# Decoder of two layers: the last joint attention's products in high and low parts, its inputs in a ring by key head

## The chip, the core and the metric

The kernel runs on one core of a Trainium2 chip. TensorE (PE) multiplies, VectorE (DVE), ScalarE (ACT) and GpSimd (POOL) work element by element, SyncE (SP) issues most of the DMAs. The metric is the device time of the whole program in microseconds, as the median of repeated runs.

## What is computed

A decoder of two layers on x of shape (8, 112, 512), each with a self-attention, an attention to a context of 375 rows per batch, and a mixture of experts. The change concerns the second layer's attention to context and own tokens together (joint attention): 16 query heads and 4 key heads of width 128, so that four query heads share a key head. Cut to what matters:

```python
kv_in = jnp.concatenate([context_hidden, draft_hidden], axis=1)      # 375 + 112 = 487 rows
q = _rope(_rms_norm(q, q_norm_w), draft_position_ids)                # (8, 16, 112, 128)
k = _rope(_rms_norm(k, k_norm_w), full_position_ids)                 # (8, 4, 487, 128)
scores = jnp.einsum('bhqd,bhkd->bhqk', q, jnp.repeat(k, 4, axis=1)) * SCALE
probs = jax.nn.softmax(scores, axis=-1)
attn = jnp.einsum('bhqk,bhkd->bhqd', probs, jnp.repeat(v, 4, axis=1))
return attn.transpose(0, 2, 1, 3).reshape(bsz, draft_len, H * HD) @ Wo.T
```

## The kernel before

The program is a row of segments. In one segment several parts run interleaved: each part is a generator per engine, and an order, written out as a list of names ("a" the attention, "o" its output product and norm, "w" the splitting of Wo), says whose next piece is issued. Every engine gets its instructions in that order and executes them in that order.

The segment "joint4" has JointAttentionPart as "a". One item is a query head (128 in all), a step takes two (W), a group is the four heads of a key head (32 in all). Each step has two half-steps. In step s, the first half-step has on TensorE the transposes (L1920) of the two heads of step s - 2 and the scores (L1928) of the two heads of step s; the second has, in odd steps, the value product of a closed group (L1940). VectorE takes in the first half-step the reciprocal of the sums (L1953), and per head the maximum (L1958) and its negative (L1960). ScalarE copies the transposed heads from PSUM (L1974, L1975) in the first and takes the exponentials (L1981) in the second half-step. GpSimd multiplies the exponentials of the step before with the reciprocals (L1907) in the first half-step. Scores and value product are plain float32, which shows in the trace as two passes for each instruction. The transposed heads alternate between two banks (N_T), so a transpose waits until the head two before it has been taken out (pt_ready). SP loads q, k and v of a whole batch ahead, into two slots each.

The output part OutNormPart ("o") takes 46 pieces, five for each batch. Four of the five hold the product of one group with Wo in high and low parts: twelve products of 512 columns (L2238, L2240, L2242). Its input is split by ScalarE (oT_hi, L2121) and VectorE (oT_lo, L2171). One piece of the five has no product but the addition to x and the statistics of the batch (L2182, L2139, L2140, L2191), another ends with the transposes of the normed rows (L2252) and their split (hT_hi, hT_lo L2159). In the order, an "o" follows the first half-step of each even step, and one more follows the second half-step of every eighth step, so TensorE has, for one group: transposes, scores, output product, transposes, scores, value product. The segment before, "p4", makes q, k and v, and loads those of the first batch at its end (FirstBatchPart).

Of the kernel before, what the change touches and what calls it, by code (L numbers as in the profile page):

```python
# [20 lines left out]
F32 = mybir.dt.float32  # L21
# [8 lines left out]
B = 8  # L30
# [1803 lines left out]
class JointAttentionPart:  # L1834


    def __init__(self, g, name, q_at, k_at, v_at, key_chunks, scale, s_banks, t_banks, o_bank, tiles):
        core, ps = g.core, g.ps
        dh, n_items, W, group = 128, 16, 2, 4
        S, nch = sum(key_chunks), len(key_chunks)  # L1840
        offs = [sum(key_chunks[:c]) for c in range(nch)]
        n_steps, n_groups = n_items // W, n_items // group
        RING, LT, LP = 3 * W, 2, 2
        LE = LP
        N_S, N_T = len(s_banks), len(t_banks)
        n_all = B * n_steps
        self.steps, self.lead, self.turned = 2 + 2 * (n_all + LE), 2 * LE, True
        q, k, v = tiles
        p = g.sb(f"{name}_p", [T, RING, S])
        pt = g.sb(f"{name}_pt", [128, 2, nch, group, T])  # L1850
# [4 lines left out]
        qk_in, v_in = g.sems(f"{name}_qk_in", 2), g.sems(f"{name}_v_in", 2)  # L1855
        s_done, mx_ready, neg_ready, exp_done, rinv_ready, p_ready, t_done, pt_ready, pv_done = (
            g.sem(f"{name}_{n}") for n in ("s_done", "mx_ready", "neg_ready", "exp_done", "rinv_ready", "p_ready", "t_done",
                                           "pt_ready", "pv_done"))
        self.ot_done, self.o_used = pv_done, None
        n_k = len(k_at(0))  # L1860
# [10 lines left out]

        def ot_view(i):
            return ps[:, o_bank, 0:group * T].rearrange("p (c t) -> p c t", c=group)
        self.ot_view = ot_view

        def sync(sp):
            yield

            def load_qk(b):
                u = b % 2  # L1880
                reuse(sp, s_done, (b - 1) * n_items)
                sp.dma_start(q[:, u, :, :], q_at(b).rearrange("(c p) t -> p c t", p=128)).then_inc(qk_in[u], 16)
# [3 lines left out]
            def load_v(b):  # L1886
                reuse(sp, pv_done, (b - 1) * n_groups)
                for c, (n, src) in enumerate(zip(key_chunks, v_at(b))):
                    sp.dma_start(v[0:n, b % 2, c, :], src).then_inc(v_in[b % 2], 16)
            yield  # L1890
            for step in range(n_all + LE):
                b, n = step // n_steps + 1, step % n_steps
                if b < B and n == (1 if b == 1 else 0):
                    load_qk(b)
                if b < B and n == LP:
                    load_v(b)
                yield
                yield

        def gpsimd(pool):  # L1900
            yield
            yield
            for step in range(n_all + LE):
                for i in items(step, 1):
                    r = i % RING
                    pool.wait_ge(rinv_ready, i // W + 1)
                    pool.tensor_tensor(p[:, r, :], p[:, r, :], rinv[:, r:r + 1].to_broadcast([T, S]), ALU.mult).then_inc(p_ready, 1)  # L1907
                yield
                yield

        def tensor(pe):
            yield
            yield
            for step in range(n_all + LE):
                for t in items(step, LT):
                    pe.wait_ge(p_ready, t + 1)
                    reuse(pe, pt_ready, t - N_T + 1)
                    for c in range(nch):
                        n = key_chunks[c]
                        last = pe.transpose(ps[0:n, t_banks[t % N_T], c * T:(c + 1) * T], p[:, t % RING, offs[c]:offs[c] + n],  # L1920
                                            core.ident[0:T, 0:T])
                    last.then_inc(t_done, 1)
                for i in items(step):
                    b, h = i // n_items, i % n_items
# [6 lines left out]
                gr = closed(step, LP, group // W)  # L1931
                if gr is not None:
                    b, j = gr // n_groups, gr % n_groups
                    if j == 0:
                        reuse(pe, v_in[b % 2], (b + 1) // 2 * 16 * nch)
                    pe.wait_ge(pt_ready, (gr + 1) * group)
                    reuse(pe, self.o_used, gr)
                    for c in range(nch):
                        n = key_chunks[c]
                        last = pe.matmul(ps[:, o_bank, 0:group * T], v[0:n, b % 2, c, j * dh:(j + 1) * dh],  # L1940
# [1695 lines left out]
```

## Time and profile before

| | |
|---|---|
| median of 3 runs | 2760.98 us (2760.76 to 2762.0) |
| profiled execution | 2759.17 us, span 2757.5 us |
| PE busy | 2506.5 us (91%) |
| DVE / ACT / POOL busy | 1666.1 (60%) / 1132.2 (41%) / 935.4 us (34%) |
| joint scores L1928, PE | 256 passes, 118.6 us, 586 ns each |
| joint value products L1940, PE | 256 passes, 102.5 us, 543 ns each |
| joint transposes L1920, PE | 512 passes, 66.0 us, 271 ns each |
| joint exponentials L1981, ACT | 128, 85.5 us, 668 ns each |

Busy time of PE overlaps: matmuls are pipelined and their ends are modelled, so starts tell more than lengths. Rows of the timeline give the start and the length in us, then engine and line, output<-inputs and the number of merged instructions, and in brackets the idle time before them and what released it.

### The profile page before, as it was taken

How to read it: one execution, taken by the hardware profiler on the slowest of the kernel's cores; microseconds unless marked ns; L12 is line 12 of the kernel's file. 1: busy time of each engine (PE TensorE's matmuls, PEld its weight loads, DVE VectorE, ACT ScalarE, POOL GpSimd, SP SyncE). 2: the span in 40 equal slices, each digit the busy share in tenths (PEclk: the TensorE clock that was granted, in tenths of full speed). 3: DMA queues.
4: the chain of work that ended last, by engine and by line, in shares of the span. 5: the costliest groups of instructions: out<-in, count | busy, mean ns of one | idle time of the engine just before them, and what ended most of it. 6: DMA issues, size and time to landing. Idle time of an engine off the chain costs nothing. (4 is left out here: it accounts for less than half of the span.)

```text
span 2757.5 us, 48350 instructions
## 1 busy us (share of the span) xinstructions
PE 2506.5 (91%) x14891; PEld 2011.7 (73%) x14892; DVE 1666.1 (60%) x3141; ACT 1132.2 (41%) x2442; POOL 935.4 (34%) x942
## 2 busy tenths in 40 slices
PE   7999788779899999799997998988999999899998
PEld 7888666558688777588875886765666577788887
DVE  4536747669677566576665566864444435666564
ACT  2113266623333234455453233755555522444343
POOL 4213101134233235323333213743333412355554
PEclk9999989989899989899998999999999989999999
DMA  5454132136521046477774432353212031666664
GB/s 190 156 143 104 27 101 71 42 98 182 170 66 55 26 136 194 150 213 217 195 220 104 127 72 84 114 172 95 86 53 92 6 129 60 171 159 157 157 161 74
DMA packets 289278, 332.88 MB, mean 121 GB/s; under 512 B 147446, under 2 KB 202694, under 8 KB 287313
## 3 DMA queue, kind: packets, MB, share of 16 engines
q1 hardware_dynamic: 217904, 252.57, 29.2%
q0 software_dynamic: 20640, 51.74, 9.6%
q10 hardware_dynamic: 50560, 26.34, 3.3%
q8 instruction: 100, 1.64, 0.2%
q14 instruction: 74, 0.60, 0.1%
HBM read 233.86 MB, written 96.72 MB: 120 GB/s over the span
## 5 line engine op out<-in xcount | busy, mean ns | idle before, releaser
L898 PE MATMUL e_psum<-e_up_hi,hT_hi 128*128 x672 | 245.9, 366 | 21.5 <-DVE hT_lo L867 16.3
L900 PE MATMUL e_psum<-e_up_hi,hT_lo 128*128 x672 | 237.2, 353 | 0.0
L899 PE MATMUL e_psum<-e_up_lo,hT_hi 128*128 x672 | 237.0, 353 | 0.0
L1907 POOL TENSOR_TENSOR joint_a_p<-joint_a_p,joint_a_rinv 112x487 f32<-112x487 f32 x128 | 125.4, 1001 | 197.8 <-DVE joint_a_rinv L1953 197.5
L1567 POOL TENSOR_TENSOR self_a_p<-self_a_p,self_a_mx 112x448 f32<-112x448 f32 x96 | 96.1, 1001 | 207.8 <-DVE self_a_mx L1624 207.8
L898 PEld LDWEIGHTS e_psum<-e_up_hi,hT_hi 128*128 128x128 f32 x672 | 127.9, 190 | 44.3 <-issue 32.7
L1958 DVE TENSOR_REDUCE joint_a_mx<-joint_psum 112x1 f32<-112x487 f32 x128 | 84.9, 664 | 122.3 <-PE joint_psum L1928 121.9
L794 ACT ACTIVATE e_gate<-e_psum 128x352 f32<-128x352 f32 (+1 forms) x86 | 44.5, 517 | 258.9 <-PE e_psum L900 258.4
L873 DVE TENSOR_TENSOR hT_lo<-e_psum,hT_hi 128x256 fp32r<-128x256 f32 (+2 forms) x138 | 55.6, 435 | 143.2 <-ACT hT_hi L812 143.2
L1658 ACT ACTIVATE self_a_p<-self_a_p 112x448 f32<-112x448 f32 x128 | 71.6, 575 | 167.7 <-POOL self_a_p L1567 114.7
L1209 POOL TENSOR_TENSOR p_p_z<-p_p_straight,p_p_crossed 128x512 f32<-128x512 f32 x70 | 98.5, 1408 | 112.3 <-DVE p_p_crossed L1191 110.4
L900 PEld LDWEIGHTS e_psum<-e_up_hi,hT_lo 128*128 128x128 f32 x672 | 127.8, 190 | 11.8
L899 PEld LDWEIGHTS e_psum<-e_up_lo,hT_hi 128*128 128x128 f32 x672 | 128.2, 191 | 9.8
L828 DVE TENSOR_TENSOR e_up_lo<-e_up_raw,e_up_hi 128x1024 f32 (+3 forms) x128 | 127.8, 1050 | 3.7 <-issue 3.4
L847 DVE SCALAR_TENSOR_TENSOR e_act_raw<-e_gate,e_rows,e_psum 128x352 f32<-128x352 f32 (+1 forms) x86 | 55.3, 644 | 121.2 <-ACT e_gate L794 119.8
L766 POOL DMA_INDIRECT out<-e_y,e_back x51 | 120.2, 2357 | 17.3 <-issue 17.3
L752 POOL TENSOR_TENSOR e_held<-e_zeros 1x1 f32<-1x1 f32 x90 | 20.8, 231 | 302.3 <-DVE e_idx L862 302.3
L898 PE MATMUL e_psum<-e_dn_hi,hT_hi 128*128 (+1 forms) x285 | 120.3, 422 | 1.3 <-issue 0.7
L1928 PE MATMUL joint_psum<-x_first,x_q 128*112 128x487 f32 x256 | 118.6, 586 | 1.8 <-PEq L89 1.7
L142 PE MATMUL p_psum<-p_p_w_hi,hT_hi 128*128 128x512 f32 x280 | 115.5, 412 | 1.9 <-DVE p_p_w_lo L1175 1.9
L1981 ACT ACTIVATE joint_a_p<-joint_psum,joint_a_neg 112x487 f32<-112x487 f32 x128 | 85.5, 668 | 76.5 <-DVE joint_a_neg L1960 73.4
L781 ACT ACTIVATE e_up_hi<-e_up_raw 128x1024 f32 (+3 forms) x128 | 107.7, 923 | 15.1 <-PEq L89 15.1
(565 smaller groups left out, 7397.1 us busy)
## 6 DMA issues: line engine op xcount, KB each, us to landing
e_up_raw<-in_L_ffn_w SPq DMA_DIRECT2D x64, 512.0 KB, 5.1
e_up_raw<-in_L_ffn_w SPq DMA_DIRECT2D x64, 352.0 KB, 3.5
e_dn_raw<-in_L_ffn_w SPq DMA_DIRECT2D x16, 1024.0 KB, 5.5
q_all<-p_p_t_stage ACTq DMA_DIRECT2D x56, 256.0 KB, 2.3
e_dn_raw<-in_L_ffn_w SPq DMA_DIRECT2D x16, 512.0 KB, 4.1
x_q<-q_all SPq DMA_DIRECT2D x8, 896.0 KB, 5.4
v_ctx<-front_c_v_stage SPq DMA_DIRECT2D x24, 250.0 KB
x_others<-k_ctx SPq DMA_DIRECT2D x8, 750.0 KB, 5.1
```

The costliest lines, as they stand in the source:

```text
L142: last = pe.matmul(out, a, b, start=(k == 0 and i == 0), stop=(k == n_k - 1 and i == len(pairs) - 1))
L766: pool.indirect_dma_start(out=acc, out_offset=bass.IndirectOffsetOnAxis(ap=back[:, v, :], axis=0), in_=y[:, v, :], in_offset=None, compute ...
L781: act.activation(up_hi[:, bass.ds(slot * KC + k, 1), :], up_raw[:, k:k + 1, :], ACT.Copy).then_inc(up_hi_ready, 1)
L828: dve.tensor_tensor(up_lo[:, bass.ds(slot * KC + k, 1), :], up_raw[:, k:k + 1, :], up_hi[:, bass.ds(slot * KC + k, 1), :].bitcast(F32), AL ...
L898: pe.matmul(out, lhs[0], rhs[0], start=k == 0, stop=False)
L899: pe.matmul(out, lhs[0], rhs[1], start=False, stop=False)
L900: return pe.matmul(out, lhs[1], rhs[0], start=False, stop=k == n_k - 1)
L1209: both = pool.tensor_tensor(z[:, r, :], straight[:, r, :], crossed[:, r, :], ALU.add)
L1567: pool.tensor_tensor(p[:, i % RING, :, :], p[:, i % RING, :, :], mx[:, i % RING, :].unsqueeze(2).to_broadcast([T, group, T]), ALU.subtract ...
L1907: pool.tensor_tensor(p[:, r, :], p[:, r, :], rinv[:, r:r + 1].to_broadcast([T, S]), ALU.mult).then_inc(p_ready, 1)
L1928: pe.matmul(ps[0:T, s_banks[i % N_S], 0:S], q[:, b % 2, h, :], k[:, b % 2, h // group, :], start=True, stop=True).then_inc(s_done, 1)
L1981: act.activation(p[:, r, :], ps[0:T, s_banks[i % N_S], 0:S], ACT.Exp, bias=neg[:, r, :], scale=scale, accum_out=rsum[:, r:r + 1]).then_inc ...
```

## The change

Scores and value products are each made of three float32r products: high x high, high x low, low x high. The high parts of q, k and v are made by ScalarE, the low parts by GpSimd (group 0's q and k by VectorE). The transposed heads get their high part from ScalarE and their low part from VectorE, in the second half-step. q, k and v are loaded per key head into rings of three slots, with high parts in rings of two. Keys are padded to 488 columns, the probabilities to 4 x 125.

```diff
+        per_group = group // W
+        RING, LT, LP, RAW, HI = 3 * W, 2, 2, 3, 2
@@ sync
+            def load_qk(gr):
+                b, j, r = gr // n_groups, gr % n_groups, gr % RAW
+                sp.wait_ge(s_done, (gr - RAW + 1) * group)
+                sp.dma_start(q[:, r, :, :], q_at(b)[j * group * dh:(j + 1) * group * dh].rearrange("(c p) t -> p c t", p=128)).then_inc(qk_in[r], 16)
                 for cols, src in k_at(b):
-                    sp.dma_start(k[:, u, :, cols], src.rearrange("(c p) t -> p c t", p=128)).then_inc(qk_in[u], 16)
+                    sp.dma_start(k[:, r, cols], src[j * dh:(j + 1) * dh]).then_inc(qk_in[r], 16)
...
+                gr = step // per_group + RAW - 1
+                if step % per_group == 0 and RAW <= gr < all_groups:
+                    load_qk(gr)
                 yield
+                gr = step // per_group + 1
+                if step % per_group == 0 and RAW <= gr < all_groups:
+                    load_v(gr)
                 yield
+        def split_qk_high(act, gr):
+            landed(act, qk_in, gr, 1 + n_k)
...
+            reuse(act, s_done, (gr - HI + 1) * group)
+            act.activation(q_hi[:, gr % HI, :, :], q[:, gr % RAW, :, :], ACT.Copy)
+            act.activation(k_hi[:, gr % HI, :], k[:, gr % RAW, :], ACT.Copy).then_inc(qk_hi_ready, 1)
+        def split_qk_low(eng, gr):
+            eng.wait_ge(qk_hi_ready, gr + 1)
+            eng.tensor_tensor(low(q[:, gr % RAW, :, :]), q[:, gr % RAW, :, :], q_hi[:, gr % HI, :, :].bitcast(F32), ALU.subtract)
+            eng.tensor_tensor(low(k[:, gr % RAW, :]), k[:, gr % RAW, :], k_hi[:, gr % HI, :].bitcast(F32), ALU.subtract).then_inc(qk_ready, 1)
...
@@ gpsimd, second half-step
+                gr = qk_at_step(step)
+                if gr is not None:
+                    split_qk_low(pool, gr)
+                gr = v_at_step(step)
+                if gr is not None:
+                    split_v_low(pool, gr)
                 yield
@@ tensor
                     if h == 0:
-                        reuse(pe, qk_in[b % 2], (b + 1) // 2 * 16 * (1 + n_k))
+                        pe.wait_ge(qk_ready, gr + 1)
                     reuse(pe, exp_done, i - N_S + 1)
-                    pe.matmul(ps[0:T, s_banks[i % N_S], 0:S], q[:, b % 2, h, :],
-                              k[:, b % 2, h // group, :], start=True, stop=True).then_inc(s_done, 1)
+                    out = ps[0:T, s_banks[i % N_S], 0:S + 1]
+                    pe.matmul(out, q_h, k_h, start=True, stop=False)
+                    pe.matmul(out, q_h, k_l, start=False, stop=False)
+                    pe.matmul(out, q_l, k_h, start=False, stop=True).then_inc(s_done, 1)
                 yield
...
+                    pe.wait_ge(v_ready, gr + 1)
                     pe.wait_ge(pt_ready, (gr + 1) * group)
                     reuse(pe, self.o_used, gr)
                     for c in range(nch):
...
+                        pe.matmul(out, v_h, p_h, start=c == 0, stop=False)
+                        pe.matmul(out, v_h, p_l, start=False, stop=False)
+                        last = pe.matmul(out, v_l, p_h, start=False, stop=c == nch - 1)
                     last.then_inc(pv_done, 1)
@@ vector
                     dve.tensor_scalar(neg[:, r, :], mx[:, r, :], -scale, None, ALU.mult).then_inc(neg_ready, 1)
                 yield
+                for t in items(step, LT):
+                    dve.wait_ge(pt_hi_ready, t + 1)
+                    dve.tensor_tensor(turned(t, pt_lo), turned_out(t), turned(t, pt_hi).bitcast(F32), ALU.subtract).then_inc(pt_ready, 1)
                 yield
@@ scalar, first half-step
-                    act.copy(to[0:key_chunks[0], 0:same, :], src[0:key_chunks[0], 0:same, :])
-                    act.copy(to[0:key_chunks[-1], same, :], src[0:key_chunks[-1], same, :]).then_inc(pt_ready, 1)
+                    act.activation(turned(t, pt_hi), turned_out(t), ACT.Copy).then_inc(pt_hi_ready, 1)
@@ scalar, second half-step, behind the exponentials
+                gr = qk_at_step(step)
+                if gr is not None:
+                    split_qk_high(act, gr)
+                gr = v_at_step(step)
+                if gr is not None:
+                    split_v_high(act, gr)
```

qk_at_step gives the next group in even steps, v_at_step the step's own group in odd ones; split_v_high and split_v_low do for v (384 and 128 columns) what the functions above do for q and k. Before the first step, ScalarE and VectorE split group 0. The first three groups' q, k and v are loaded in "p4", where the old loads of the first batch were.

## Rows read from the trace of the kernel before

**Rows 1.** Page, part 2: granted TensorE clock in 40 slices, tenths.

```profile
PEclk9999989989899989899998999999999989999999
```

**Rows 2.** Busy by stretch: length; PE, PEld, DVE, ACT, POOL (count); clock, DMA, GB/s.

```profile
2034.00:2078.40 44.40, 43.51 (x182) 27.08 (x181) 18.65 (x50) 22.94 (x69) 16.18 (x17) 1.00 0.24 72
```

**Rows 3.** Timeline of one batch, PE: start, length (us), engine, line, operands.

```profile
1990.28 3.17 PE L1940 MATMUL joint_psum<-joint_a_pt,x_v 125*128 125x448 f32 x8
...
1993.29 1.00 PE L1920 MATMUL joint_psum<-ident,joint_a_p 112*125 112x112 f32 x8
...
1996.44 0.39 PE L2238 MATMUL joint_psum<-joint_wo_hi,joint_o_oT_hi 128*112 128x512 f32 x1
...
1997.14 0.40 PE L2238 MATMUL joint_psum<-joint_wo_hi,joint_o_oT_hi 128*112 128x512 f32 x1
...
2002.55 1.80 PE L1928 MATMUL joint_psum<-x_first,x_q 128*112 128x487 f32 x4
...
2004.19 3.17 PE L1940 MATMUL joint_psum<-joint_a_pt,x_v 125*128 125x448 f32 x8
```

**Rows 4.** Timeline, PE, fp32r passes of 448 columns; nine such passes lie between.

```profile
199.92 0.36 PE L1455 MATMUL self_psum<-hT_hi,x_first_lo 128*128 128x448 f32 x1
...
201.95 0.36 PE L1455 MATMUL self_psum<-hT_hi,x_first_hi 128*128 128x448 f32 x1
```

**Rows 5.** Timeline of the same batch, DVE, with idle time before and releaser.

```profile
1995.96 0.67 DVE L1958 TENSOR_REDUCE joint_a_mx<-joint_psum 112x1 f32<-112x487 f32 x1
...
1996.73 0.61 DVE L2171 TENSOR_TENSOR joint_o_oT_lo<-joint_psum,joint_o_oT_hi 128x448 fp32r<-128x448 f32 x1
...
2002.48 0.62 DVE L2159 TENSOR_TENSOR hT_lo<-joint_psum,hT_hi 128x448 fp32r<-128x448 f32 x1 [5.14 <-ACT hT_hi L2124]
...
2003.02 0.16 DVE L1953 RECIPROCAL joint_a_rinv<-joint_a_rsum 112x2 f32<-112x2 f32 x1
...
2003.57 0.67 DVE L1958 TENSOR_REDUCE joint_a_mx<-joint_psum 112x1 f32<-112x487 f32 x1 [0.40 <-PE joint_psum L1928]
...
2004.39 0.67 DVE L1958 TENSOR_REDUCE joint_a_mx<-joint_psum 112x1 f32<-112x487 f32 x1
```

**Rows 6.** Groups by line, 1848 to 2226 us: busy us, mean ns | idle before.

```profile
L1907 POOL TENSOR_TENSOR joint_a_p<-joint_a_p,joint_a_rinv 112x487 f32<-112x487 f32 x128 | 125.4, 1001 | 197.8 <-DVE joint_a_rinv L1953 197.5
...
L2171 DVE TENSOR_TENSOR joint_o_oT_lo<-joint_psum,joint_o_oT_hi 128x448 fp32r<-128x448 f32 x32 | 19.7, 615 | 8.8 <-ACT joint_o_oT_hi L2121 8.8
...
L2121 ACT ACTIVATE joint_o_oT_hi<-joint_psum 128x448 fp32r<-128x448 f32 x32 | 18.5, 578 | 3.4 <-PE joint_psum L1940 3.4
...
L2139 DVE BATCH_NORM_STATS2 joint_o_stats<-x_tok 112x6 f32<-112x512 f32 x8 | 5.6, 694 | 0.7
...
L2182 DVE TENSOR_TENSOR x_tok<-joint_psum,x_tok 112x512 f32<-112x512 f32 x8 | 5.5, 681 | 1.6 <-PE joint_psum L2242 1.6
...
L2140 DVE BATCH_NORM_AGGREGATE joint_o_mv<-joint_o_stats 112x2 f32<-112x6 f32 x8 | 1.5, 182 | 0.3
...
L2191 DVE TENSOR_SCALAR joint_o_var_eps<-joint_o_mv 112x1 f32<-112x1 f32 x8 | 1.2, 153 | 0.3
```

**Rows 7.** Idle stretches (timeline), and busy time and clock behind them (stretches).

```profile
418.43 0.90 PE L1742 MATMUL cross_psum<-x_others 32*112 32x375 f32 x8 [2.31 <-ACT cross_a_p L1825]
...
418.50:421.90 3.40, 3.33 (x34) 2.53 (x38) 3.26 (x7) 2.14 (x7) 0.00 (x0) 1.00 0.00 0
...
441.82 1.61 PE L1742 MATMUL cross_psum<-x_others 32*112 32x375 f32 x8 [2.30 <-ACT cross_a_p L1825]
...
441.80:445.80 4.00, 3.98 (x19) 2.92 (x20) 3.51 (x8) 0.98 (x3) 0.00 (x0) 0.50 0.00 0
...
1872.59 1.06 ACT L2010 ACTIVATE joint_wo_hi<-joint_w_raw 128x1024 fp32r<-128x1024 f32 x1 [4.79 <-DMA joint_w_raw<-in_L_xattn_Wo]
...
1876.11 1.16 PE L1920 MATMUL joint_psum<-ident,joint_a_p 112*125 112x112 f32 x4 [5.20 <-POOL joint_a_p L1907]
...
1876.00:1879.40 3.40, 3.29 (x10) 2.37 (x11) 2.12 (x4) 3.20 (x9) 1.01 (x2) 0.50 0.39 143
```

More of the change, by code:

```diff
@@ L1839, in __init__ @@
         dh, n_items, W, group = 128, 16, 2, 4
-        S, nch = sum(key_chunks), len(key_chunks)
-        offs = [sum(key_chunks[:c]) for c in range(nch)]
+        S, nch, rows = sum(key_chunks), len(key_chunks), max(key_chunks)
         n_steps, n_groups = n_items // W, n_items // group
-        RING, LT, LP = 3 * W, 2, 2
+        per_group = group // W
+        RING, LT, LP, RAW, HI = 3 * W, 2, 2, 3, 2
         LE = LP
         N_S, N_T = len(s_banks), len(t_banks)
-        n_all = B * n_steps
+        n_all, all_groups = B * n_steps, B * n_groups
         self.steps, self.lead, self.turned = 2 + 2 * (n_all + LE), 2 * LE, True
-        q, k, v = tiles
-        p = g.sb(f"{name}_p", [T, RING, S])
-        pt = g.sb(f"{name}_pt", [128, 2, nch, group, T])
+        q, k, v, v_hi = tiles
+        q_hi = g.sb(f"{name}_q_hi", [128, HI, group, T], F32R)
+        k_hi = g.sb(f"{name}_k_hi", [128, HI, S + 1], F32R)
+        p = g.sb(f"{name}_p", [T, RING, nch * rows])
+        pt_hi, pt_lo = (g.sb(f"{name}_pt_{part}", [128, 2, nch, group, T], F32R) for part in ("hi", "lo"))
         neg = g.sb(f"{name}_neg", [T, RING, 1])
@@ L1870, in closed, with qk_at_step, v_at_step, landed @@
             return at // per if 0 <= at < n_all and at % per == per - 1 else None
+        def qk_at_step(step):
+            gr = step // per_group + 1
+            return gr if step % per_group == 0 and gr < all_groups else None
+        def v_at_step(step):
+            gr = step // per_group
+            return gr if step % per_group == per_group - 1 and gr < all_groups else None
+        def landed(eng, sems, gr, per_load):
+            reuse(eng, sems[gr % RAW], 16 * per_load * (gr // RAW))
+        def low(tile):
+            return tile.bitcast(F32R)
         def ot_view(i):
@@ new lines, in split_v_high, with split_v_low @@
+        def split_v_high(act, gr):
+            landed(act, v_in, gr, nch)
+            reuse(act, pv_done, gr - HI + 1)
+            for raw, hi in v_parts(gr):
+                last = act.activation(hi, raw, ACT.Copy)
+            last.then_inc(v_hi_ready, 1)
+        def split_v_low(eng, gr):
+            eng.wait_ge(v_hi_ready, gr + 1)
+            for raw, hi in v_parts(gr):
+                last = eng.tensor_tensor(low(raw), raw, hi.bitcast(F32), ALU.subtract)
+            last.then_inc(v_ready, 1)
@@ L1900, in gpsimd @@
         def gpsimd(pool):
             yield
+            pool.memset(k[:, :, S:S + 1], 0.0).then_inc(padded, 1)
+            pool.memset(p[:, :, S:nch * rows], 0.0)
             yield
@@ L1918, in tensor @@
                     for c in range(nch):
-                        n = key_chunks[c]
-                        last = pe.transpose(ps[0:n, t_banks[t % N_T], c * T:(c + 1) * T], p[:, t % RING, offs[c]:offs[c] + n],
+                        last = pe.transpose(ps[0:rows, t_banks[t % N_T], c * T:(c + 1) * T], p[:, t % RING, c * rows:(c + 1) * rows],
                                             core.ident[0:T, 0:T])
@@ L1939, in tensor, with turned, turned_out @@
                         n = key_chunks[c]
-                        last = pe.matmul(ps[:, o_bank, 0:group * T], v[0:n, b % 2, c, j * dh:(j + 1) * dh],
-                                         pt[0:n, gr % 2, c, :, :].rearrange("p h t -> p (h t)"), start=(c == 0), stop=(c == nch - 1))
+                        p_h, p_l = (t[0:n, gr % 2, c, :, :].rearrange("p h t -> p (h t)") for t in (pt_hi, pt_lo))
+                        v_h, v_l = v_hi[0:n, gr % HI, c, :], low(v[0:n, gr % RAW, c, :])
+                        out = ps[:, o_bank, 0:group * T]
+                        pe.matmul(out, v_h, p_h, start=c == 0, stop=False)
+                        pe.matmul(out, v_h, p_l, start=False, stop=False)
+                        last = pe.matmul(out, v_l, p_h, start=False, stop=c == nch - 1)
                     last.then_inc(pv_done, 1)
                 yield
+        def turned(t, tile):
+            return tile[0:rows, t // group % 2, :, t % group, :]
+        def turned_out(t):
+            return ps[0:rows, t_banks[t % N_T], 0:nch * T].rearrange("p (i t) -> p i t", i=nch)
         def vector(dve):
             yield
+            split_qk_low(dve, 0)
             yield
```

71 lines of the change are left out of this document (36 added, 35 removed).

## The prediction

> **What bounds the kernel now.** I read the page first for where the clock stands [rows 1], then the busy time of the joint segment, some 377 us long, from 1849 to 2226 us. In its steady part TensorE works 43.5 of 44.4 us, the period of one batch, at the full clock (2.4 GHz); VectorE has 18.7, ScalarE 22.9 and GpSimd 16.2 us in the same stretch [rows 2]. So TensorE sets the pace, and the others have room. The timeline gives what each piece really occupies, from start to start: a busy figure counts the pipeline's tail twice. Two scores are four passes from 2002.55 to 2004.19, so 0.82 us for one head; a group's value product is eight passes from 1990.28 to 1993.29, so 3.01 us [rows 3]. The output product, already in three parts, starts its triples 0.70 us apart, so 0.233 us for a pass of 512 columns [rows 3], and passes of 448 columns of the same kind follow each other at (201.95 - 199.92) / 10 = 0.203 us [rows 4].
>
> **TensorE gets less work.** One head's scores become three passes of 488 columns. No row has that width; it lies between 0.203 and 0.233 us [rows 3, 4], and in proportion to the columns 0.222, so 0.67 us for 0.82 (0.61 to 0.70). A value product becomes twelve passes of 448 columns, 12 x 0.203 = 2.43 us for 3.01 (up to 2.80). Per batch of 16 heads and 4 groups: 16 x 0.155 + 4 x 0.58 = 4.8 us less, 38 us over 8 batches. The transposes stay (the last chunk is 125 wide for 112, a few ns). Were this all, the kernel would win 1.4%.
>
> **VectorE comes between scores and values.** Before, a value product waits for a ScalarE copy that runs beside the scores; in all TensorE loses 44.4 - 43.5 = 0.9 us a batch [rows 2]. Now pt_ready comes from VectorE's subtraction, and VectorE takes it in the second half-step, behind the reductions of both heads scored in this same step. An engine works in order: VectorE sat 5.14 us in front of hT_lo for its input [rows 5], with all behind it waiting. In the odd step nothing of the output part lies between scores and value product, for TensorE goes from the one at 2002.55 straight to the other at 2004.19 [rows 3]. So, with 0 where TensorE could begin the value product: the first head's scores end at -0.67; their reduction begins 0.20 later (2003.57 against 2002.55 + 0.82 [rows 3, 5]), at -0.47; the second 0.82 later (2003.57 to 2004.39 [rows 5]), at 0.35; the subtraction for the first head 0.77 after that (1995.96 to 1996.73 [rows 5]), at 1.12; that for the second 0.54 later (2002.48 to 2003.02 [rows 5]), at 1.66; it lasts 0.62 [rows 6], and 0.05 for the signal gives 2.33 us of idle TensorE in each of 32 groups. Bounds: 1.8 if the signals are quicker and the subtractions overlap more, 2.8 if two of these are slower. 4 x 2.33 less the 0.9 lost today is 8.4 us a batch.
>
> **A second wait per batch.** A transpose in an odd step overwrites the bank of the even step's, whose subtraction must be done. In three of four groups the output part (12 x 0.233 = 2.8 us) covers this: the subtraction of the first head would end at 1.12 + 0.55 (oT_lo) + 0.67 = 2.34. In the fourth there is no output product in between, and VectorE does there the batch's addition and statistics first: 1.12 + 0.68 + 0.69 + 0.18 + 0.15 [rows 6] + 0.55 + 0.67 = 4.0 us, and 0.1 for the second head. I take 4.1 (3.5 to 4.5). Per batch -4.8 + 8.4 + 4.1 = +7.7; times 8 is **+61 us** after rounding.
>
> **The rest.** ScalarE's added high parts (448 and 488, then 384 and 128 columns; by 0.58 for 448 [rows 6] about 2 us a group) stand behind its exponentials; with 22.9 + 4 x 2 of 52 us it keeps room, and its one copy of 448 columns is at most 0.1 us slower than the two it replaces. GpSimd's low parts are 1448 columns a group, by 1.00 us for 487 [rows 6] 3.0 us or, if a plain second operand is dearer than the broadcast one, up to 3.7. Its normalisation is queued behind them: the second exponential starts with VectorE's last signal at about 1.1 and takes 0.67 (table), high parts 1.2, low parts of q and k 2.5, two products 2.0 and signals 0.2, together 7.7 us after the even step's scores; the next group's transposes come after output product 2.8, transposes 0.8 (1.00 less a tail of 0.16, as 0.39 is to 0.233 [rows 3]), scores 1.3, wait 2.3 and value product 2.4, so 9.6 us. It costs nothing, with 1.9 us to spare. The prologue splits q and k ahead of the first score: about 0.6 + 0.6 on ScalarE, then 0.6 + 0.65 on VectorE, 2 us; the groups at the start and end that have no output product to cover the bank's wait add some 4: **+6** (0 to 10). SP's loads come four times as often with a quarter of the bytes; they are waited for a step before use, and issue beside work. At the start ScalarE stood 4.79 us for a piece of Wo and TensorE 5.20 us behind it [rows 7], while the second batch's loads were in flight; these are now small: **-5** (0 to -8). In the first segment the same first loads go into other tiles: 0 (-1 to +1).
>
> **The clock.** After 5.20 us without work TensorE ran at 1.2 GHz through the next 3.4 us; in the cross attention the same idle of 2.3 us was followed once by full clock and once by half [rows 7]. 3.4 us of dense work at half clock loses 1.7. With half of the 32 short waits and nearly all of the 8 long ones followed so, 16 x 1.7 + 8 x 1.7 = 41 at most; some of these stretches reach into the next wait, so I take **+35** (0 to 68, all 40). The Trainium skill, page "TensorE: Matmul & The Clock Gate", section "HAM oscillation — how this bites in real kernels", warns of long pauses alone and would pass the short ones: by it the term is that of the long ones, 8 x 1.7 = 14, and the time some 21 us lower. The trace's second short pause, followed by half clock, speaks against reading it so strictly.
>
> **The sum.** 61 + 6 - 5 + 35 = +97. The profiled execution took 2759.2 us (span 2757.5, 1.7 around it), the median of the runs is 2761.0; on the median the forecast is 2761 + 97 = **2858 us**.
>
> **Rivals.** (B) The clock holds through all waits, as it did once [rows 7]: 2858 - 35 = 2823. (C) It falls after every wait, twice as long after the long ones: 40 x 1.7 + 8 x 1.7 = 82 for 35, so 2905. (D) GpSimd becomes the bound: the spare 1.9 us are gone once its 4.5 us of low parts and products take over 42% longer. At 1.8 times the 7.7 us become 11.3, 1.7 over, in three groups of four: 5 us a batch, 41 in all, so 2899. The Trainium skill, page "GPSIMD Engine Reference", section "Specifications", says that it shares its SBUF interfaces with VectorE, with contention where VectorE reads two SBUF inputs; in the segment of before the products kept to 1.00 us [rows 6], and the new subtraction reads one operand from PSUM. (E) **Faster**: VectorE's subtractions are covered, as its load (18.7 of 44.4 us [rows 2]) would allow, were the order of its queue to leave them ahead of the reductions or output work to stand before the value product. Then 38 + 7 (the 0.9 a batch) + 5 - 2 of prologue are won: 2713. It decides where the added waits per group come below (38 + 7 + 5) / 32 = 1.6 us. Against it stands the written order: each subtraction is issued after both reductions, and these cannot begin before their scores end. (F) The products don't get cheap as said: every new pass takes 0.233. Then 128 x 0.033 + 32 x 0.36 = 16 of the 38 are lost: 2874.
>
> **Chances.** Forecast 0.55; B 0.14; C 0.08; D 0.05; E 0.10, of which 0.03 end within 0.2%; F 0.08. The forecast, B, F and the near side of C and D, with the bounds of the terms, give 2812 to 2888; by that about 0.2 is outside. What a measurement of this kernel can tell from no change is about 0.2%, 5.5 us. Slower by more 0.90, within 0.03, faster 0.07.
>
> **What would show it.** Right: TensorE idle in front of the value product about 32 times for 2.3 us, released by VectorE's pt_lo; once a batch some 4 us in front of a transpose; batches 52 us apart plus the clock; the granted clock near 0.9 from 1900 us on; score passes 0.22 us apart. Wrong: a wait under 1.6 us or a release by ScalarE (E), GpSimd's joint_a_p in front of transposes (D), granted clock 1.00 (B), or under 0.8 (C).

## The result, and the profile after

The changed kernel took 2880.49 us in the median of 4 runs (2873.86 to 2881.18), the kernel before 2760.87 in the same comparison: 1.0431 times as long, interval 1.0419 to 1.0444, so 119.6 us more. The forecast was 2858 with a range of 2812 to 2888. The profiled execution took 2881.18 us, 122.0 more than that of before. I date the joint segment by its first score and by the next segment's first product: 1853.25 to 2353.18 us, 499.9 us, against 1848.97 to 2228.27, 379.3 us, before. The added time lies there.

The page of after: busy time by engine, and the granted clock of TensorE in 40 slices (tenths), where [rows 1] is the line of before.

```profile
PE 2537.2 (88%) x15147; PEld 2106.2 (73%) x15148; DVE 1732.3 (60%) x3271; ACT 1178.1 (41%) x2442; POOL 1059.9 (37%) x1070
...
PEclk9999899899999899899989989888898879999999
```

Busy time by stretch, after (columns as in [rows 2]): the first 52 us of the segment, then 300 us of its steady part.

```profile
1848.00:1900.00 52.00, 31.10 (x119) 24.39 (x118) 27.26 (x55) 29.25 (x63) 29.64 (x28) 0.74 0.39 124
1900.00:2200.00 300.00, 236.88 (x1061) 193.51 (x1060) 135.23 (x333) 145.51 (x349) 159.87 (x169) 0.86 0.19 52
```

TensorE was busy 98% of a batch in [rows 2] at clock 1.00; now it is 79%, at 0.86, and no other engine comes near the length of the stretch. It waits, and it runs at 1.2 GHz for part of the rest. Whom it waits for, waits view of after, 1848 to 2340 us (us in total, times, longest):

```profile
DVE joint_a_mx L2034 <- PE joint_psum L1996: 212.1, 68, 7.0
...
PE joint_psum L2008 <- issue: 67.2, 31, 3.5
...
PE joint_psum L1983 <- DVE joint_a_pt_lo L2040: 33.9, 10, 4.0
```

The second row is the value product (L2008), 31 times 2.17 us on average. "issue" hides the releaser; the two timelines of one step show it. PE, after, start and length in us:

```profile
2052.55 0.38 PE L1996 MATMUL joint_psum<-joint_a_k_hi,x_first 128*112 128x488 f32 x1
2052.76 0.38 PE L1994 MATMUL joint_psum<-joint_a_k_hi,joint_a_q_hi 128*112 128x488 f32 x1
2052.98 0.38 PE L1995 MATMUL joint_psum<-x_first,joint_a_q_hi 128*112 128x488 f32 x1
2053.20 0.39 PE L1996 MATMUL joint_psum<-joint_a_k_hi,x_first 128*112 128x488 f32 x1
2055.76 0.44 PE L2008 MATMUL joint_psum<-joint_a_pt_hi,x_first 125*128 125x448 f32 x1 [2.17 <-issue]
2056.04 0.37 PE L2009 MATMUL joint_psum<-joint_a_pt_lo,x_first 125*128 125x448 f32 x1
...
2057.96 0.57 PE L2008 MATMUL joint_psum<-joint_a_pt_hi,x_first 112*128 112x448 f32 x1
2058.34 0.57 PE L2009 MATMUL joint_psum<-joint_a_pt_lo,x_first 112*128 112x448 f32 x1
```

DVE, after, the same step:

```profile
2052.96 0.67 DVE L2034 TENSOR_REDUCE joint_a_mx<-joint_psum 112x1 f32<-112x487 f32 x1 [0.26 <-PE joint_psum L1996]
2053.66 0.15 DVE L2036 TENSOR_SCALAR joint_a_neg<-joint_a_mx 112x1 f32<-112x1 f32 x1
2053.74 0.67 DVE L2034 TENSOR_REDUCE joint_a_mx<-joint_psum 112x1 f32<-112x487 f32 x1
2054.44 0.15 DVE L2036 TENSOR_SCALAR joint_a_neg<-joint_a_mx 112x1 f32<-112x1 f32 x1
2054.51 1.15 DVE L2040 TENSOR_TENSOR joint_a_pt_lo<-joint_psum,joint_a_pt_hi 125x448 fp32r<-125x448 f32 x2
```

The scores end at 2053.59. Each reduction follows the scores of its head, the second one ends at 2054.41; the two subtractions run from 2054.51 to 2055.66, and 0.10 us later the value product begins. Behind its first pass (0.28 us) the passes start some 0.20 us apart, those from 2057.96 on 0.38: the clock has fallen. The granted clock says the same. Stretches of after, from the value product on (busy time of PE behind the length; the clock is third from the end):

```profile
2055.76:2057.20 1.44, 1.44 (x7) 1.35 (x8) 0.00 (x0) 0.24 (x2) 1.12 (x2) 1.00 0.55 171
2057.20:2060.60 3.40, 3.40 (x15) 3.17 (x14) 0.00 (x0) 0.47 (x1) 2.23 (x3) 0.51 0.03 10
2060.60:2067.20 6.60, 6.59 (x34) 5.00 (x33) 3.86 (x9) 4.52 (x11) 2.14 (x2) 0.99 0.11 34
```

So here a pause of 2.17 us was followed, after 1.4 us of dense work, by 3.4 us at half clock with TensorE busy all the way.

**A measure for what follows.** A batch's period is read from one start to the next of the first transposes of the normed rows (L2334 in after), over five batches: 60.05 us after (1989.61 to 2289.86), 44.46 before (1956.92 to 2179.20). Eight times the difference is 124.7 us, all of the loss; start and end give back some 5.

### The profile page after: what moved, and what is told of

Read it like the earlier page. It is cut to its first block and busy times, and to the rows that moved or that the text cites. A ratio compares the mean times of both kernels' runs of the same rounds, so it can differ in the third digit from the quotient of the medians.

```text
span 2879.5 us, 49352 instructions
## 1 busy us (share of the span) xinstructions
PE 2537.2 (88%) x15147; PEld 2106.2 (73%) x15148; DVE 1732.3 (60%) x3271; ACT 1178.1 (41%) x2442; POOL 1059.9 (37%) x1070
## 3 DMA queue, kind: packets, MB, share of 16 engines
q8 instruction: 102, 1.67, 0.2%
## 5 line engine op out<-in xcount | busy, mean ns | idle before, releaser
L2051 ACT ACTIVATE joint_a_pt_hi<-joint_psum 125x448 fp32r<-125x448 f32 x128 | 65.4, 543 | 162.6 <-PE joint_psum L1983 161.9
L2008 PE MATMUL joint_psum<-joint_a_pt_hi,x_first 125*128 125x448 f32 (+1 forms) x128 | 63.6, 497 | 69.3 <-issue 67.2
L1983 PEld LDWEIGHTS joint_psum<-ident,joint_a_p 112*125 112x125 f32 x512 | 82.3, 232 | 49.0 <-issue 38.0
```

What stands on the lines that cost most here:

```text
L1983: last = pe.transpose(ps[0:rows, t_banks[t % N_T], c * T:(c + 1) * T], p[:, t % RING, c * rows:(c + 1) * rows], core.ident[0:T, 0:T])
```

## The experiments

Each is an edit of the changed kernel, timed together with the kernel before; times are medians. The ratio of an experiment goes by the runs of the kernel before that were timed with it (medians 2759.59 to 2760.17), not by the 2760.87 of the first row. The period is the one just defined, the clock is that of 1900 to 2200 us.

| kernel | us | ratio to before (95%) | period | clock |
|---|---|---|---|---|
| before | 2760.87 | 1 | 44.46 | 1.00 |
| after | 2880.49 | 1.0431 (1.0419 to 1.0444) | 60.05 | 0.86 |
| e1_lo_first | 2764.71 | 1.0013 (1.0003 to 1.0022) | 43.37 | 0.99 |
| e2_values_later | 2773.18 | 1.0043 (1.0026 to 1.0061) | 45.62 | 0.95 |
| e4_fill | 2828.02 | 1.0246 (1.0228 to 1.0264) | 53.00 | 1.00 |
| e7_no_gpsimd_low | 2877.91 | 1.0424 (1.0391 to 1.0456) | 60.07 | 0.86 |
| e5_scores_only | 2752.50 | 0.9972 (0.9960 to 0.9983) | 43.37 | 1.00 |
| e6_values_only | 2884.47 | 1.0449 (1.0432 to 1.0466) | 61.69 | 0.88 |
| e3_later_lo_half1 | 2754.15 | 0.9979 (0.9967 to 0.9991) | 42.17 | 0.98 |
| e8_first_group_plain | 2748.33 | 0.9962 (0.9949 to 0.9976) | 42.17 | 0.98 |
| e9_scores_later_plain0 | 2753.83 | 0.9979 (0.9970 to 0.9990) | 42.83 | 1.00 |
| e10_start | 2751.72 | 0.9974 (0.9962 to 0.9986) | 42.17 | 0.98 |
| e11_rings_only | 2756.80 | 0.9987 (0.9978 to 0.9996) | 44.62 | 1.00 |

**e1_lo_first: only VectorE's order.** If the loss comes from the subtraction standing behind the reductions, moving it ahead must remove it.

```diff
@@ vector, first half-step
                     dve.reciprocal(rinv[:, r:r + W], rsum[:, r:r + W]).then_inc(rinv_ready, 1)
+                for t in items(step, LT):
+                    dve.wait_ge(pt_hi_ready, t + 1)
+                    dve.tensor_tensor(turned(t, pt_lo), turned_out(t), turned(t, pt_hi).bitcast(F32), ALU.subtract).then_inc(pt_ready, 1)
                 for i in items(step):
@@ vector, second half-step
-                for t in items(step, LT):
-                    dve.wait_ge(pt_hi_ready, t + 1)
-                    dve.tensor_tensor(turned(t, pt_lo), turned_out(t), turned(t, pt_hi).bitcast(F32), ALU.subtract).then_inc(pt_ready, 1)
```

> VectorE's two subtractions (pt_lo) are issued in the first half-step, ahead of the two reductions of the same step instead of behind them; nothing else differs from the changed kernel. Theory (the order of VectorE's queue makes TensorE wait, and the waits pull the clock down): the second subtraction ends about 2.3 us after the transposes, beside 2.2 us of transposes' tail and scores, so the wait of 2.16 us before each value product falls under 0.7 us, the 4.0 us once a batch vanish, the granted clock returns to 0.97 or more in the joint part, and a batch takes some 44 us: 2765 us in all (2745 to 2790). Rival (the new passes, the loads in small pieces or GpSimd's low parts cost the time, the order does not): within 20 us of the 2880 of the changed kernel.

It took 2764.71: three lines moved give back 116 us of 120. It is not faster than before, though: the period is 1.09 us shorter, but the joint segment of the profiled execution takes 380.2 us for 379.3, so what eight periods gain, 8.7 us, goes again at the start, where waits of 3.12, 4.29 and 4.29 us stand ahead of the first value products. DVE of this kernel, one step: the subtractions now run while TensorE computes the scores, with the reductions behind.

```profile
1961.34 1.16 DVE L2032 TENSOR_TENSOR joint_a_pt_lo<-joint_psum,joint_a_pt_hi 125x448 fp32r<-125x448 f32 x2 [1.31 <-ACT joint_a_pt_hi L2051]
1962.41 0.66 DVE L2037 TENSOR_REDUCE joint_a_mx<-joint_psum 112x1 f32<-112x487 f32 x1
```

One wait per batch is left, in the group without an output product (PE, this kernel):

```profile
1995.71 0.44 PE L2008 MATMUL joint_psum<-joint_a_pt_hi,x_first 125*128 125x448 f32 x1 [1.55 <-DVE joint_a_pt_lo L2032]
```

**e2_values_later: only TensorE's order.** The value product comes one step later, behind an even step's output product.

```diff
-        RING, LT, LP, RAW, HI = 3 * W, 2, 2, 3, 2
+        RING, LT, LP, RAW, HI = 3 * W, 2, 3, 3, 2
```

> The constant LP is 3 instead of 2: a group's value product is issued one step later, so that both subtractions of that group were issued in the step before. The order of VectorE's queue stays. Theory of the queue: the wait before the value product disappears, about 2 us of wait per batch before a transpose stay, GpSimd's products come close to binding, a batch takes some 43 us at full clock: 2755 us (2735 to 2785). Rival (GpSimd is the bound once TensorE waits no longer for VectorE): waits for joint_a_p of over 1 us per group, 2790 or more. Rival (the time does not lie in the order): near 2880.

It took 2773.18, 18 more than expected. The short waits are gone, but the long one, for the transposes' bank, is as it was (3.95 to 4.02 us, seven times), and the clock of 0.95 shows that it alone costs clock as well: behind each of the seven came half clock. PE, this kernel:

```profile
1943.61 1.99 PE L1983 MATMUL joint_psum<-ident,joint_a_p 112*125 112x112 f32 x8 [3.96 <-DVE joint_a_pt_lo L2040]
```

**e4_fill: the clock by itself.** Products that nobody reads stand where TensorE would wait: 9 of 488 columns ahead of each value product and, from the second batch on, 17 ahead of the transposes that wait long. The waits' length stays, the pauses go.

```diff
+                def fill(n, i, gr, done):
+                    reuse(pe, exp_done, done)
+                    for _ in range(n):
+                        pe.matmul(ps[:, s_banks[i % N_S], 0:S + 1], k_hi[:, gr % HI, 0:128], k_hi[:, gr % HI, :], start=True, stop=True)
+                if step % 2 == 1 and (step - 3) // 2 % 4 == 2 and step > 14 and items(step):
+                    fill(17, items(step)[0], items(step)[0] // group, items(step)[0] - N_S + 1)
...
+                    if items(step):
+                        fill(9, items(step)[-1] + 1, items(step)[0] // group, items(step)[0])
```

> The waits stay, but TensorE runs unneeded products during them (9 passes of 488 columns before each value product, 17 before the transposes that wait 4 us, into a bank that the next scores overwrite; their results are not used). Theory (the waits themselves cost about 60 us and half-rate clock after every one of them another 60): granted clock 0.98 or more in the joint part, batch period 52 us instead of 60, total 2818 us (2808 to 2832), though TensorE gets more work. Rival (the lower clock is harmless because TensorE waits anyway, all 120 us are the waits): 2880 or above.

More work on the engine that sets the pace made the kernel 52 us faster. Stretch and PE timeline of this kernel:

```profile
1900.00:2200.00 300.00, 295.85 (x1502) 242.41 (x1501) 150.24 (x373) 162.69 (x393) 176.01 (x187) 1.00 0.22 61
```

```profile
2032.20 2.15 PE L1982 MATMUL joint_psum<-joint_a_k_hi 128*128 128x488 f32 x9
2034.55 0.44 PE L2016 MATMUL joint_psum<-joint_a_pt_hi,x_first 125*128 125x448 f32 x1 [0.19 <-issue]
```

The period is 53.00 us at clock 1.00. Between the first score of a step and its value product lie 3.73 us (2030.82 to 2034.55), in after 3.72 (2052.04 to 2055.76), and between the scores and the transposes that wait long 5.50 to 5.58 in both, so the fill stands in for the wait and lengthens nothing. This splits the loss: 8.5 us of period are waits less the cheaper products, 7.05 are the clock; 67.9 us (2828.02 less the 2760.17 of the kernel before, timed with it) and 52.5 us of the total.

**e7_no_gpsimd_low: is GpSimd a bound?** Its low parts of q, k and v shrink to one column each, so their true low parts are missing from the products; output and time are to be read so. The same function makes group 0's low parts on VectorE, so these shrink too, and the wait ahead of the first score falls from 4.78 to 3.74 us. Nothing else moves.

```diff
-            eng.tensor_tensor(low(q[:, gr % RAW, :, :]), q[:, gr % RAW, :, :], q_hi[:, gr % HI, :, :].bitcast(F32), ALU.subtract)
-            eng.tensor_tensor(low(k[:, gr % RAW, :]), k[:, gr % RAW, :], k_hi[:, gr % HI, :].bitcast(F32), ALU.subtract).then_inc(qk_ready, 1)
+            eng.tensor_tensor(low(k[:, gr % RAW, S:S + 1]), k[:, gr % RAW, S:S + 1], k_hi[:, gr % HI, S:S + 1].bitcast(F32), ALU.subtract).then_inc(qk_ready, 1)
...
-                last = eng.tensor_tensor(low(raw), raw, hi.bitcast(F32), ALU.subtract)
+                last = eng.tensor_tensor(low(raw[:, 0:1]), raw[:, 0:1], hi[:, 0:1].bitcast(F32), ALU.subtract)
```

> GpSimd's low parts of q, k and v are left out but for a sliver that keeps the signals (so the output is not the reference's): 4 us of GpSimd's work per group less. Theory of VectorE's queue: no change, 2880 us (within 6). Rival (GpSimd's queue is a bound of the changed kernel): 10 us or more faster.

2877.91, intervals overlapping those of after, the same period. GpSimd's busy time falls by 40% (159.87 us in the same stretch of after) and nothing follows:

```profile
1900.00:2200.00 300.00, 235.97 (x1053) 193.18 (x1053) 133.33 (x332) 144.14 (x346) 96.53 (x146) 0.86 0.19 53
```

**e5_scores_only and e6_values_only: one part alone.** e5 keeps the value products in plain float32, with ScalarE's copy releasing them as before; e6 keeps the scores plain. The rings stay in both. The core of e5:

```diff
-                        pe.matmul(out, v_h, p_h, start=c == 0, stop=False)
-                        pe.matmul(out, v_h, p_l, start=False, stop=False)
-                        last = pe.matmul(out, v_l, p_h, start=False, stop=c == nch - 1)
+                        last = pe.matmul(ps[:, o_bank, 0:group * T], v[0:n, gr % RAW, c, :],
+                                         pt[0:n, gr % 2, c, :, :].rearrange("p h t -> p (h t)"), start=c == 0, stop=c == nch - 1)
...
-                for t in items(step, LT):
-                    dve.wait_ge(pt_hi_ready, t + 1)
-                    dve.tensor_tensor(turned(t, pt_lo), turned_out(t), turned(t, pt_hi).bitcast(F32), ALU.subtract).then_inc(pt_ready, 1)
```

and that of e6:

```diff
-                    pe.matmul(out, q_h, k_h, start=True, stop=False)
-                    pe.matmul(out, q_h, k_l, start=False, stop=False)
-                    pe.matmul(out, q_l, k_h, start=False, stop=True).then_inc(s_done, 1)
+                    pe.matmul(ps[0:T, s_banks[i % N_S], 0:S], q[:, gr % RAW, h, :], k[:, gr % RAW, 0:S], start=True, stop=True).then_inc(s_done, 1)
```

> Of the change, the scores in three products, with the rings; the value products are plain float32 again, with ScalarE's two copies and no subtraction on VectorE. Theory of VectorE's queue: no wait between scores and values, clock at 1.00 after the first groups; 16 x 0.155 = 2.5 us less per batch, 20 in all, against some 10 us that the split ahead of the first score and the slow clock behind it cost: 2751 us (2740 to 2762). Rival (the splits of q and k on ScalarE and GpSimd, or the scores' passes, cost time of their own): above 2765.

> Of the change, the value products in three products, with the rings; the scores are plain float32 again, without splits of q and k and without the split ahead of the first score. Theory of VectorE's queue: the waits are those of the whole change (about 2.2 and 4.0 us, four and one a batch), with the slow clock behind them, and the scores' 20 us are not won: 2890 us (2875 to 2905), worse than the whole change. Rival (the two parts share the loss): between 2790 and 2850.

The loss is whole in e6 (2884.47) and absent from e5 (2752.50, 8 us faster than before). PE of e5, one step at full clock from the first score to the value product:

```profile
1956.29 0.45 PE L1991 MATMUL joint_psum<-joint_a_k_hi,joint_a_q_hi 128*112 128x488 f32 x1
1956.58 0.38 PE L1992 MATMUL joint_psum<-x_first,joint_a_q_hi 128*112 128x488 f32 x1
1956.80 0.38 PE L1993 MATMUL joint_psum<-joint_a_k_hi,x_first 128*112 128x488 f32 x1
...
1957.68 0.54 PE L2002 MATMUL joint_psum<-joint_a_pt,x_v 125*128 125x448 f32 x1
```

Two heads take 1.39 us, 1.64 before [rows 3]; passes are 0.22 apart, but the first one behind the transposes takes 0.29. PE of e6, the wait ahead of the value product:

```profile
2052.37 0.65 PE L2000 MATMUL joint_psum<-joint_a_pt_hi,x_first 125*128 125x448 f32 x1 [2.05 <-issue]
```

**e3_later_lo_half1: both orders at once.** e2's later value product, and the subtractions in the first half-step, directly behind the reductions. That puts them ahead of the output part's VectorE work, which made e2's long wait long.

```diff
-        RING, LT, LP, RAW, HI = 3 * W, 2, 2, 3, 2
+        RING, LT, LP, RAW, HI = 3 * W, 2, 3, 3, 2
@@ vector, behind the reductions
-                yield
                 for t in items(step, LT):
                     dve.wait_ge(pt_hi_ready, t + 1)
...
+                yield
```

> The value product one step later (LP = 3), and VectorE's two subtractions directly behind the reductions, at the end of the first half-step, so ahead of the output part's work on VectorE; their place behind the reductions stays. Theory: the wait of 3.95 us once a batch before a transpose, left when only the value product is moved, falls to 1.8 us or less, with the slow clock behind it: batches near 42 us where it was 45.0, total 2750 us (2738 to 2762), faster than before the change. Rival (GpSimd's queue binds now): waits for joint_a_p take its place, 2765 or more.

2754.15, the period 42.17 us. The long wait has shrunk from 3.96 to 1.69 (PE):

```profile
1942.59 0.66 PE L1983 MATMUL joint_psum<-ident,joint_a_p 112*125 112x112 f32 x4 [1.69 <-DVE joint_a_pt_lo L2039]
```

Eight periods gain 18 us, of which the total shows 6. The profiled executions put most of the missing 12 at the start: from the last product of "p4" to the first of the next segment e3 takes 374.0 us (1849.42 to 2223.41), before 381.4 (1846.90 to 2228.27), 7.4 less instead of 18.

**e8_first_group_plain: the prologue.** e3, with group 0's scores in plain float32, so nothing is split ahead of the first score. Its edit, against e3:

```diff
+                    if gr == 0:
+                        pe.matmul(ps[0:T, s_banks[i % N_S], 0:S], q[:, 0, h, :], k[:, 0, 0:S], start=True, stop=True).then_inc(s_done, 1)
+                        continue
...
-            split_qk_low(dve, 0)
...
-            split_qk_high(act, 0)
```

> As the kernel with the later value product and the subtractions in the first half-step, but the scores of group 0 are plain float32, so that no split stands ahead of the first score. Theory (the start of the segment costs by the 4.78 us without work and the half-rate clock that begins there): the idle stretch is 1.7 us, the clock holds, the first group is done some 5 to 8 us earlier: 6 us less than the kernel without this edit (3 to 9). Rival (only the idle stretch counts): 3 us or less.

2748.33, 5.8 less than e3 and the lowest median of all: 0.9962 of before (0.9949 to 0.9976), 10 to 12 us. The wait ahead of the first score fell from 4.78 us to the 1.69 that before has too. Behind it stands a wait for GpSimd's joint_a_p of 5.02 us (5.58 in e3, 3.23 in before). Whether more than the idle stretch was won is open: the intervals of e3 and e8 overlap, and from the last product of "p4" to the next segment the profiled e8 takes 370.4 us, 3.6 less than e3, of which 3.1 are that stretch.

**e9_scores_later_plain0: the best pieces together?** High and low parts for the scores only, with e8's later value product and plain group 0. The edit is e5's and e8's together.

> Scores in three products, value products plain float32 (so no subtraction on VectorE), the value product one step later (LP = 3), and the scores of group 0 plain float32. Theory: against the kernel with the scores alone the wait of 1.64 us once a batch before a value product goes (13 us over 8 batches) and the start costs 6 us less: 2735 us (2726 to 2745), the fastest of all, since a batch then has no wait on VectorE at all. Rival (the GpSimd queue binds as soon as TensorE is quicker than 43 us a batch): 2745 to 2755, with waits for joint_a_p.

A miss: 2753.83, no better than e5. The wait for ScalarE's copy (1.65 us once a batch in e5) is gone, but only a third of it came back, 0.54 us of period. This lies in the range that the expectation gave to its rival, GpSimd's queue. The next thing late is GpSimd's normalisation, once a batch by 0.97 to 1.00 us, and by 5.03, 4.80 and 3.90 us in the first 50 us, where e5 has one such wait above 1 us, of 4.58. PE, this kernel:

```profile
1940.71 0.69 PE L1980 MATMUL joint_psum<-ident,joint_a_p 112*125 112x112 f32 x4 [0.99 <-POOL joint_a_p L1965]
```

**e10_start: the rest of the start.** e8, with the subtractions ahead of the reductions in the first ten steps, and group 1's low parts of q and k made by VectorE. Against e8:

```diff
@@ vector, ahead of the reductions
+                if step < 10:
+                    for t in items(step, LT):
+                        dve.wait_ge(pt_hi_ready, t + 1)
...
-                if gr is not None:
+                if gr is not None and gr > 1:
                     split_qk_low(pool, gr)
...
+                if step == 0:
+                    split_qk_low(dve, 1)
```

> As the kernel with the later value product, the subtractions at the end of the first half-step and group 0 plain; in addition, in the first ten steps VectorE takes the subtractions ahead of the reductions, and splits group 1 itself in place of GpSimd. Theory (in the first batch nothing of the output product covers VectorE's queue, and GpSimd's first split delays its first normalisation): the 5.0 us wait of the start falls by 2.5 us and the waits of 1.6 to 2.4 us for pt_lo in the first groups nearly go: 2741 us (2734 to 2748). Rival (the weight splits on ScalarE and VectorE bind in the first batch): no change, 2748.

A miss too: 2751.72, within its interval no different from e8; in the profiled executions the stretch from the last product of "p4" to the next segment is 3.2 us longer than e8's (373.6 for 370.4). TensorE's waits of the first 50 us are now all for GpSimd's joint_a_p (waits view, 1847 to 1900 us; the row of the weight loads, PEld, overlaps the other):

```profile
PEld joint_psum L1983 <- POOL joint_a_p L1965: 18.9, 6, 5.0
PE joint_psum L1983 <- POOL joint_a_p L1965: 15.9, 6, 4.5
```

Whether GpSimd's queue or the chain ahead of it (reduction, exponential, reciprocal) makes joint_a_p late there I did not separate. In e7, with hardly any low parts to make, the first such wait was still 3.77 us, against 4.57 in after and 3.23 in before. So most of it was there without any low part, but of the 1.3 us that the change added, 0.8 went with them.

**e11_rings_only: loads and padding alone.** Rings, 488 columns and 4 x 125 stay; all products are plain float32.

> Of the change, the loads per key head into rings of three alone (with the padding of keys and probabilities); all products plain float32, no splits. Theory as in the prediction's term for the loads: smaller loads beside the pieces of Wo at the start, -3 us (-8 to +2): 2757 us. Rival (loads in four times as many and smaller pieces, queued on SyncE, hold up the segment): 2765 or more, with waits for DMA.

2756.80, 3 us faster (1 to 6 by the interval). The period is even 0.16 us longer, so the gain lies at the start: TensorE's wait of 5.20 us [rows 7] behind the queued loads is gone.

## Why the prediction was right, and where it was not

**What bounds the kernel; the work saved.** Right. Two heads' scores take 1.39 us (predicted 1.34) and a value product 2.50 (2.43): there is a little extra at each change from one kind of product to the next, which a spacing read inside a row of like passes does not hold. Transposes got 0.04 us shorter, 0.79 for 0.83. By these, 8 x 0.25 + 4 x 0.51 + 8 x 0.04 gives 4.4 us less a batch; predicted 4.8.

**The wait before the value product.** Right in place, cause and size: the idle field shows 2.17 us, counted from the modelled end of the last pass; from the place where the value product could have started (1.39 us behind the first score) it is 2.33, as predicted. The chain of two reductions and two subtractions came out link by link. That the rows call it "issue" for want of a semaphore in the record is no matter: e1 moves VectorE's three lines and of four such waits a batch one of 1.6 us is left.

**The second wait.** Right in place and size: 3.94 to 4.01 us ahead of a transpose, predicted 4.1. It came seven times, not eight: the first batch has three shorter ones instead (1.57, 2.21 and 2.21). PE of after:

```profile
2018.49 0.66 PE L1983 MATMUL joint_psum<-ident,joint_a_p 112*125 112x112 f32 x4 [3.94 <-DVE joint_a_pt_lo L2040]
```

Counted by starts, as above, it is 4.2 (5.57 us from first score to transposes, for 1.39). So 2.33 us are lost four times a batch and 4.2 once. Less the 0.9 of before and the 4.4 of cheaper products that is 8.2; e4 measured 8.5, predicted were 7.7 (times 8 that is 61.6; the prediction wrote 61).

**Start, end and loads.** +6 and -5 were predicted, 1 us in all. In e4, whose early pauses before transposes are not filled, the total over eight periods is 0 (67.9 against 8 x 8.5), so the sum holds, in part by luck: eight periods count eight long waits, and seven came. The prologue cost 3.1 us (4.78 for 1.69), 2 predicted. The smaller loads gave back 3 in e11, whose interval (1 to 6) holds the predicted 5. The start weighs more once the waits are gone: e3 loses some 11 us there.

**The clock: the mis-sized term.** The failed step is "With half of the 32 short waits and nearly all of the 8 long ones followed so". It rested on two short pauses in [rows 7], one of each kind. In after 27 of the 32 value products took longer than 2.6 us, for 2.50 at full clock. The granted clock around each wait tells them apart. Of the 25 waits of 2.05 to 2.17 us ahead of a value product that began at full clock, 21 were followed by half clock, and so was one of 3.45; in five more the clock was at half before the wait began, and the last wait, of 1.43, had none behind it. All seven long waits were followed by half clock, and behind four of them it lasted 10.24 us, through the next short wait and the value product behind it (the other of the five lies in the first batch). One of the four, stretches and PE timeline of after:

```profile
2019.73:2029.97 10.24, 8.19 (x25) 6.66 (x24) 2.77 (x7) 2.93 (x8) 5.73 (x7) 0.50 0.18 48
...
2024.02 0.71 PE L2008 MATMUL joint_psum<-joint_a_pt_hi,x_first 125*128 125x448 f32 x1 [2.06 <-issue]
```

TensorE worked 8.2 us of that stretch, so it lost 4.1. In place of 16 x 1.7 + 8 x 1.7 = 41 belongs, as an estimate from these counts, 22 x 1.7 + 3 x 1.7 + 4 x 4.1 = 59. Measured by e4: **52 us for 35**, or 1.3 us for each of some 40 waits. The term's bounds of 0 and 68 held it. The terms without the clock were 62 and came out at 67.9; the clock was 35 and came out at 52.5; together 120.3 for 97. Both were too low, so no error hid another. And e4 does not fill the start: in its first 50 us there TensorE still worked 19.8 us at half clock, where before has 8.8. Half of the difference, 5.5, is an estimate of clock that is left in the 67.9; by it the terms without the clock come to 62, as predicted, and the clock to 58.

The Trainium skill, page "TensorE: Matmul & The Clock Gate", section "HAM oscillation — how this bites in real kernels", speaks of long pauses alone. This case's rows differ: waits of 2.05 to 2.17 us that began at full clock were followed by half clock 21 times in 25, and filling these and the long ones brought clock 1.00 and 52 us. The measurement decides.

**The rivals.** (B), the clock holds: refuted, 0.86. (C), it falls after every wait, twice as long after the long ones: the measured 2880 lies halfway between it and the forecast. Four of the seven long waits did cost twice or more, but four short ones of the 25 brought no half clock and three long ones cost only once; its 82 us stand against 52 to 58. (D), GpSimd: refuted by e7 for the changed kernel. Its low parts did cost more than I allowed, as the groups of after from 1848 to 2340 us show (us busy, mean ns), 1.14 + 1.36 + 1.02 + 0.59 = 4.1 us a group for 3.0 to 3.7:

```profile
L1936 POOL TENSOR_TENSOR x_first<-x_first,joint_a_k_hi 128x488 fp32r<-128x488 f32 x31 | 42.1, 1359 | 0.0
L1935 POOL TENSOR_TENSOR x_first<-x_first,joint_a_q_hi 128x448 fp32r<-128x448 f32 x31 | 35.4, 1142 | 134.7 <-ACT joint_a_k_hi L1931 134.7
L1953 POOL TENSOR_TENSOR x_v<-x_v,x_first 125x384 fp32r<-125x384 f32 x32 | 32.5, 1016 | 38.0 <-ACT x_first L1947 37.8
...
L1953 POOL TENSOR_TENSOR x_v<-x_v,x_first 112x128 fp32r<-112x128 f32 x32 | 18.8, 586 | 0.0
```

The products stayed at 999 ns, so nothing in the segment shows GpSimd slowed by its neighbours. (E), the subtractions are covered: refuted for this order, and true for another. e3 and e8 reach a period of 42.17, where E's 2713 would want about 38.8 (44.4 less 45 / 8); what is missing in the period is a wait of 1.69 us, the clock behind some of these waits (0.98), and a rest that no run separates; in the total, the start too. (F), passes no cheaper: refuted for most; 0.22 apart.

## What to carry to other kernels

Splitting operands for cheaper passes puts one more element-wise step between two products. Its price is set less by the engine's load (VectorE was busy 45% of the time) than by where the step stands in that engine's queue: put it ahead of whatever waits for TensorE's newest result. Where the pacing engine will pause every few microseconds, price the clock for each pause, not for the long ones only. A saving in the steady part is worth what is left after the start: of 18 us in e3, 6 arrived.

## What was unexpected of the hardware

Pauses as short as 2.17 us, in a part that was otherwise dense, were followed by half clock (21 of 25), in the batch shown 1.4 us after the pause had ended and for 3.4 us with TensorE fully busy. With one pause of 4 us in each batch they brought the granted clock from 1.00 to 0.86 over 300 us. One pause of 1.55 to 1.69 us a batch did far less: in e1 none of the seven (1.55 to 1.63) was followed by half clock, and its 0.99 comes from the stretch's first 12 us; in e3 three of the seven (1.68 and 1.69) were, one of them with a second pause of 1.67 just behind it (0.98). Adding unneeded products to TensorE, 53 a batch, made the program 52 us shorter.
